# Convolution weights loaded in one order of the phases, the other order copied across the partition halves by ScalarE

## What is computed

```
t1 = p1_w * x ;  t2 = x + t1 ;  t4 = relu(x)
t5 = unfold(x, 3 x 7 taps, padding 1, 3)              # (n, c, 21, h, w)
t7 = einsum('oc,nchw->nohw', p7_w, t4)
t8 = unfold(t7, 1 x 5 taps, dilation 3, padding 6)
t9 = x[:, :, None] - t8
t10 = grouped 1x1 convolution of t2 by p10_w (4 groups, 32 -> 672 channels each)
t11 = einsum('nck,nmk->ncm', t1, t5) / sqrt(h * w)
t12 = t9.mean(2)
t13 = einsum('ncm,nmk->nck', t11, t10) / sqrt(c * 21)
out = maximum(t13, t12)
```

## Time and profile before

| | |
|---|---|
| median of 3 runs | 400.69 us (400.04 to 400.71) |
| the profiled execution | 400.21 us |
| its span, first to last instruction | 398.4 us |
| outside the span | 1.8 us |
| mean granted TensorE clock | 0.997 |
| TensorE, VectorE, ScalarE, GpSimd busy | 98%, 82%, 62%, 21% of the span |
| moved by DMA | 90.76 MB, 228 GB/s over the span |

### The profile page before, as it was taken

The page is one execution under the profiler, slowest core; times in us unless marked ns, Lnnn a source line. Parts: engine busy times, 40 slices in busy tenths (PEclk is TensorE's granted clock), DMA queues, the critical chain, the costliest instruction groups (busy, mean ns, idle before and its releaser), DMA issues.

```text
span 398.4 us, 10378 instructions
## 1 busy us (share of the span) xinstructions
PE 388.6 (98%) x4104; PEld 170.9 (43%) x4104; DVE 328.7 (82%) x395; ACT 249.0 (62%) x714; POOL 84.1 (21%) x72
## 2 busy tenths in 40 slices
PE   7999999999999999999999999999999999999995
PEld 3222653435633364333833337333553337332373
DVE  5988969988987897878978789787878789787625
ACT  1053547776577673776556773777727766578870
POOL 0442000522022221222022220222202222222200
PEclk9999999999999999999999999999999999999998
DMA  8999408893767949677566848579395783643205
GB/s 314 405 408 410 164 2 319 311 332 111 266 214 252 332 133 302 200 253 249 191 219 249 286 158 252 180 265 324 126 318 176 250 282 107 214 133 108 79 3 212
DMA packets 28705, 90.76 MB, mean 228 GB/s; under 512 B 3312, under 2 KB 3568, under 8 KB 28656
## 3 DMA queue, kind: packets, MB, share of 16 engines
q1 hardware_dynamic: 28656, 90.09, 64.1%
HBM read 73.30 MB, written 16.78 MB: 226 GB/s over the span
## 4 chain that ended last, share of the span: by engine, by line
PE 87%; ACT 4%; DVE 3%; DMA 2%; issue 2%; SPq 1%; DVEq 0%; ACTq 0%
PE ps_y L731 40%; PE ps_y L816 13%; PE ps_p L753 12%; PE ps_t L753 12%; PE ps_y L742 8%; ACT t L335 3%; DMA xw<-x_conv 2%; PE ps_y L753 2%; ACT base L273 1%; DVE yT L543 1%; DVE base L584 0%; DVE pair_sum L553 0%; SPq L170 0%; DVE box L561 0%; DVE box L570 0%
## 5 line engine op out<-in xcount | busy, mean ns | idle before, releaser
L731 PE MATMUL ps_y<-v_planes,u_planes 64*64 64x512 f32 x1536 | 193.0, 596 | 1.7 <-issue 0.7
L242 POOL TENSOR_TENSOR t1T<-t1T,p1T_sb 128x512 f32<-128x512 f32 x60 | 76.4, 1296 | 277.3 <-PE ps_y L742 245.4
L335 ACT ACTIVATE t<-xn,p_plus 128x64 f32<-128x64 f32 x512 | 128.0, 334 | 0.0
L753 PE MATMUL ps_p<-box,p_fifth 64*64 64x512 f32 x456 | 117.3, 590 | 0.5 <-DVE box L570 0.5
L753 PE MATMUL ps_t<-t,aT 64*64 64x512 f32 x448 | 115.4, 591 | 0.1
L731 PEld LDWEIGHTS ps_y<-v_planes,u_planes 64*64 64x64 f32 x1536 | 56.2, 132 | 116.3 <-issue 98.2
L273 ACT ACTIVATE base<-ps_p 128x512 f32<-128x512 f32 x57 | 34.0, 597 | 76.5 <-PE ps_p L753 76.1
L584 DVE TENSOR_TENSOR base<-ps_t,base 128x512 f32<-128x512 f32 x56 | 38.5, 688 | 27.9 <-PE ps_t L753 27.8
L816 PEld LDWEIGHTS ps_y<-t1T,yT 128*128 128x128 f32 x512 | 57.8, 192 | 6.5 <-issue 5.7
L816 PE MATMUL ps_y<-t1T,yT 128*128 128x128 f32 x512 | 59.3, 277 | 0.0
L543 DVE STREAM_TRANSPOSE yT<-ps_y 128x512 f32<-128x512 f32 x64 | 42.0, 695 | 17.5 <-PE ps_y L742 17.5
(11 more groups left out here) (43 smaller groups left out, 148.0 us busy)
## 6 DMA issues: line engine op xcount, KB each, us to landing
xw<-x_conv SPq DMA_DIRECT2D x64, 561.0 KB, 6.5
xn<-x_nat SPq DMA_DIRECT2D x32, 512.0 KB, 4.6
t1T<-x_pix SPq DMA_DIRECT2D x32, 512.0 KB, 6.8
out<-base SPq DMA_DIRECT2D x64, 256.0 KB, 4.9
u_planes<-w_tiles SPq DMA_DIRECT2D x4, 672.0 KB, 8.6
p1T_sb<-p1T SPq DMA_DIRECT2D x1, 128.0 KB, 10.7
p_sb<-p7T SPq DMA_DIRECT2D x1, 64.0 KB, 10.7
p_sb<-p SPq DMA_DIRECT2D x1, 32.0 KB, 11.0
```

The lines of the kernel that those rows point to most:

```text
L242: nc.gpsimd.tensor_tensor(part, part, p1T_sb[:, e, :].unsqueeze(1).broadcast_to([P, 4, C]), ALU.mult).then_inc(t1_ready, 1)
L335: last = nc.scalar.activation(t2[:, h, W * r:W * (r + 1)], xn[:, f, at:at + W], ACT.Copy, scale=p1_plus[:, 8 * h + r:8 * h + r + 1])
L731: last = nc.tensor.matmul(dst[TILE * pair:TILE * pair + TILE, :], weights_of(rows_of(half), u, weights, TILE * k, TILE), data_of(rows_of(h ...
L753: last = nc.tensor.matmul(dst[cols, 0:data.shape[-1]], weights[rows, cols], data[rows, :], start=start, stop=False, skip_group_check=True)
```

## The change

The weights come from memory in the FRONT order alone, three rows a group, into planes 0 to 2 of six (`U_0`, `U_2`, `OUTER`). `weights` makes three sums of 224 elements: `U_1` (as scratch) = r0 + r2, `U_1_FRONT` = that + r1, and `U_2` = that - r1, the last now behind a wait of its own. Then ScalarE copies the planes `OUTER` and `U_1_FRONT` of each half of the partitions into the planes `U_3` and `U_1` of the other half: two copies of 64 partitions x 448 elements a group (`swap`). TensorE waits for the copies (`u_swapped`) and no longer for the sums. One of the warm-up matmuls becomes half as long.

```diff
-U_0, U_2, U_1, U_3 = (FRONT, 0), (FRONT, 1), (BACK, 1), (BACK, 2)
+U_0, U_2, OUTER, U_1_FRONT, U_3, U_1 = range(6)
-        u_planes = sb("u_planes", [P, GROUPS, 2, KH, WCOLS])
+        u_planes = sb("u_planes", [P, GROUPS, 6, WCOLS])
-                sp.dma_start(u_planes[:, g], w_tiles[g]).then_inc(w_loaded[g], 16)
+                sp.dma_start(u_planes[:, g, 0:KH, :], w_tiles[g]).then_inc(w_loaded[g], 16)
...
-                both = u_planes[:, g].rearrange("p o r c -> p (o r) c")
-                nc.vector.tensor_tensor(both[:, 2:4], both[:, 0:4:3], both[:, 2:6:3], ALU.add).then_inc(u_steps, 1)
+                u = u_planes[:, g]
+                nc.vector.tensor_tensor(u[:, U_1], u[:, U_0], u[:, OUTER], ALU.add).then_inc(u_steps, 1)
                 dve.wait_ge(u_steps, U_STEPS * g + 1)
-                nc.vector.tensor_tensor(both[:, 4], both[:, 3], both[:, 4], ALU.add).then_inc(u_steps, 1)
-                nc.vector.tensor_tensor(both[:, 1], both[:, 2], both[:, 1], ALU.subtract).then_inc(u_steps, 1)
+                nc.vector.tensor_tensor(u[:, U_1_FRONT], u[:, U_1], u[:, U_2], ALU.add).then_inc(u_steps, 1)
+                dve.wait_ge(u_steps, U_STEPS * g + 2)
+                nc.vector.tensor_tensor(u[:, U_2], u[:, U_1], u[:, U_2], ALU.subtract).then_inc(u_steps, 1)
...
+            def swap(g):
+
+                if g < 2:
+                    act.wait_ge(u_steps, U_STEPS * (g + 1))
+                else:
+                    act.wait_ge(u_later, U_STEPS * (g - 1))
+                for half in range(2):
+                    copy(u_planes[TILE * half:TILE * half + TILE, g, U_3:U_1 + 1, :],
+                         u_planes[TILE - TILE * half:P - TILE * half, g, OUTER:U_1_FRONT + 1, :]).then_inc(u_swapped, 1)
...
+            swap(0)
+            swap(1)
             copy_two(0)
+            swap(2)
             copy_two(1)
             act.wait_ge(small_loaded, SMALL)
             copy(p7_fifth[:], p7_sb[:], FIFTH).then_inc(p7_scaled, 1)
             relu(0, 0)
+            swap(3)
             seed_x(0, 0)
...
-                        pe.wait_ge(u_steps, U_STEPS * (u + 1))
                     else:
                         pe.wait_ge(v_ready, 3 * u + 2)
-                        if u < GROUPS:
-                            pe.wait_ge(u_later, U_STEPS * (u - 1))
+                    if u < GROUPS:
+                        pe.wait_ge(u_swapped, 2 * u + 2)
...
-            for bank_set in (ps_p7[:, 0:HALF // 2], ps_t13, ps_p7, ps_p7):
+            for bank_set in (ps_p7[:, 0:HALF // 2], ps_p7[:, 0:HALF // 2], ps_t13, ps_p7):
```

More of the change, by code:

```diff
@@ L122, in conv_seq_kernel @@
         u_later = sem("u_later")
+        u_swapped = sem("u_swapped")
         v_ready = sem("v_ready")
@@ L247, in weights @@
                 pool.wait_ge(w_loaded[g], 16)
-                both = u_planes[:, g].rearrange("p o r c -> p (o r) c")
-                nc.gpsimd.tensor_tensor(both[:, 2:4], both[:, 0:4:3], both[:, 2:6:3], ALU.add).then_inc(u_later, 1)
+                u = u_planes[:, g]
+                nc.gpsimd.tensor_tensor(u[:, U_1], u[:, U_0], u[:, OUTER], ALU.add).then_inc(u_later, 1)
                 pool.wait_ge(u_later, U_STEPS * (g - 2) + 1)
-                nc.gpsimd.tensor_tensor(both[:, 4], both[:, 3], both[:, 4], ALU.add).then_inc(u_later, 1)
-                nc.gpsimd.tensor_tensor(both[:, 1], both[:, 2], both[:, 1], ALU.subtract).then_inc(u_later, 1)
+                nc.gpsimd.tensor_tensor(u[:, U_1_FRONT], u[:, U_1], u[:, U_2], ALU.add).then_inc(u_later, 1)
+                pool.wait_ge(u_later, U_STEPS * (g - 2) + 2)
+                nc.gpsimd.tensor_tensor(u[:, U_2], u[:, U_1], u[:, U_2], ALU.subtract).then_inc(u_later, 1)
             nc.gpsimd.memset(v_planes[:, :, :, 0:BLOCKS_PAD:BLOCKS_PAD - 1, :], 0.0).then_inc(edges_zeroed, 1)
@@ L719, in weights_of @@
             def weights_of(rows, u, plane, at, width):
-                order, row = plane
-                return u_planes[rows, u % GROUPS, order, row, at:at + width]
+                return u_planes[rows, u % GROUPS, plane, at:at + width]
             def data_of(rows, u, plane, block):
@@ L982, in weight_tiles @@
     w = p10.reshape(GROUPS, CG, KH, KW, CG)
-    out = np.zeros((GROUPS, P, 2, KH, WCOLS), p10.dtype)
+    out = np.zeros((GROUPS, P, KH, WCOLS), p10.dtype)
     for g in range(GROUPS):
-        for order in range(2):
-            for quarter, phase in enumerate(PHASES_OF[g % 2, order]):
-                rows = slice(CG * quarter, CG * quarter + CG)
-                for k, (pair, at) in enumerate(DENSE[phase <= 2]):
-                    for s in range(2):
-                        tap = phase + PHASES * (at - 1) - (2 * pair + s)
-                        out[g, rows, order, :, TILE * k + CG * s:TILE * k + CG * s + CG] = w[g, :, :, tap]
-                to, at = SINGLE[phase]
-                out[g, rows, order, :, 3 * TILE:] = w[g, :, :, phase + PHASES * (at - 1) - to]
+        for quarter, phase in enumerate(PHASES_OF[g % 2, FRONT]):
+            rows = slice(CG * quarter, CG * quarter + CG)
+            for k, (pair, at) in enumerate(DENSE[phase <= 2]):
+                for s in range(2):
+                    tap = phase + PHASES * (at - 1) - (2 * pair + s)
+                    out[g, rows, :, TILE * k + CG * s:TILE * k + CG * s + CG] = w[g, :, :, tap]
+            to, at = SINGLE[phase]
+            out[g, rows, :, 3 * TILE:] = w[g, :, :, phase + PHASES * (at - 1) - to]
     return out
```

## The result

With the change the kernel takes 398.84 us (median of 6 runs, 398.73 to 399.26), beside 400.41 us (median of 6) for the kernel before. The ratio is 0.9961, with a 95% interval of 0.9949 to 0.9974: about 1.6 us less, and faster by more than 0.2%. The profiled execution took 398.83 us against 400.21, with a span of 397.0 us against 398.4.

The account below looks back on a forecast made before the run. TensorE, busy 98%, was taken as the limit, its start bound by transferred bytes; 0.85 us at unit 0 plus 0.16 at unit 1 made 1.01 us off the 400.69 median: 399.7 us, range 398.9 to 400.6.

Parts of the forecast that it names:

- What bounds the start: First 20 us: TensorE's start waits on transfers and is bound by bytes, at 379 to 411 GB/s.
- The sums and copies, at nothing: VectorE sums end at 5.10, ScalarE's first copies at 6.2 us; the eight copies' 4.5 us fit idle time, costing nothing.
- The bytes, 0.85 us: One halved weight load ahead of unit 0's last data transfer brings that data 0.85 us earlier; upper bound 0.91.
- It does not hold up 7.64: Shortened warm-up leaves TensorE free at 7.26 us, so it does not delay unit 0's start at 7.64.
- Unit 0's term: Start of unit 0: TensorE begins its first weight load 0.85 us earlier.
- Unit 1's wait, 0.16 us: Start of unit 1: TensorE's 0.16 us of waiting for VectorE disappears as well.
- So nothing more is won: After the start: earlier transfers bring no further gain, since vector engines hardly wait for transfers from 14 to 62 us.
- moves with it: Later units: the vector engines' work is released by TensorE and shifts along with TensorE's earlier start.
- Rival 2: After unit 3 an engine not moving with TensorE ends last, gain given back: no change, 400.6 us; chance 0.12.
- The basis: Whole kernel: the gain was subtracted from 400.69 us, the median of the runs before, giving 399.7 us.
- Rival 1 and 3: Start: ramp or late clock trims gain, about 400.1 us (0.22); much later clock rise, slower (0.06, including a late copy).

Follow-up runs that it names:

- e1: Changed kernel with every weight load back at all six planes (672 KB); 400.43 us, ratio 1.0008 against the kernel before.
- e5: Changed kernel with only group 0's weight load at full 672 KB; median 400.05 us, ratio 1.0008 against the kernel before.
- e11: Changed kernel with only the weight loads of groups 2 and 3 at full size; 399.28 us, ratio 0.9965 against the kernel before.
- e7: Changed kernel with two more pairs of ScalarE copies, into a scratch buffer, ahead of each pair; 400.17 us, ratio 0.9998.
- e8: Changed kernel with 256 fewer warm-up columns and unit 0's last transfer and sum split into 9 and 8 blocks; 399.38 us, ratio 0.9989.
- e4: Changed kernel with another 256 columns of warm-up removed; 399.11 us, ratio 0.9973 against the kernel before.
- e2: Changed kernel with the longer warm-up of the kernel before (256 columns more); 399.37 us, ratio 0.9976.
- e3: Kernel before with only the shorter warm-up of the change; median 400.29 us, ratio 1.0008.
- e6: Changed kernel with only group 1's weight load at full size; 399.93 us, ratio 0.9983 against the kernel before.
- e10: Changed kernel with group 1's weight load moved behind the first half of unit 1's data; 399.57 us, ratio 0.9980.
- e12: Changed kernel with only group 0's weight load at full size and the long warm-up of before; 400.10 us, ratio 0.9991.
- e9: Changed kernel unaltered, timed again in a later series; 399.26 us, ratio 0.9968 against the kernel before.
- e18: Changed kernel with GpSimd's first two product pairs for image 1 released at other points, between VectorE's sums; 398.05 us, ratio 0.9944.

## Why the prediction was wrong, point by point

- **What bounds the start: right.** e1, e5 and e11 show that the gain is the bytes ahead of units 0 and 1 and nothing else; the chain's DMA share went from 2% to none.
- **The sums and copies, at nothing: right.** Forecast ends of 5.10 and 6.2, measured 5.08 and 6.29; two copies took 1.17 us against 1.1. GpSimd's sums were over at 15.15 (forecast 14.6 to 17.7). e7 shows the cover: about 1.05 us.
- **The bytes, 0.85 us: too small, and taken for one number.** V_1 began 1.09 us earlier (7.69 to 6.60). By the landings of the 16 parts, the first came 0.81 earlier (6.87 to 6.06), the eighth 0.94 (7.15 to 6.21) and the last 1.09 (7.67 to 6.58). The rate gave the first rightly; what VectorE waits for is the last. How much earlier the last comes isn't fixed by one pair of profiles: over all profiles but e8's, it came at 7.61 to 8.06 us with the full first load (7 profiles, middle one 7.77) and at 6.47 to 7.77 with the half (12 profiles, median 7.00), which is 0.77 between the medians, while the mean of the 16 parts came 0.96 earlier. So 1.09 is that of a good draw, and the sum below holds for this pair.
- **"It does not hold up 7.64" (the warm-up): too optimistic by a little.** It was to end at 7.26, and start unit 0 with V_1 at 7.64. Data came earlier than I thought, and then the warm-up did hold unit 0, by 0.06 us (e4). Unit 0's term is 1.03 us, not 0.85.
- **Unit 1's wait, 0.16 us: 0.24.** I took 1.08 us from the singles to the next unit out of later units; behind unit 0, which has half as many of them, it is 1.02 (10.67 to 11.69). The sum of the two terms is 1.27 us instead of 1.01.
- **"So nothing more is won", and it "moves with it": wrong.** 0.12 us more were won, at 70 us, where GpSimd's products met VectorE's sums otherwise. The fourteen profiles with the products at their place sort by one number, how long before `pair_sum` they start: from 0.02 us before it to 0.36 behind (the changed kernel, e2, e3, e5, e6, e7, e10, e11) `pair_sum` takes 1.31 or 1.32 us and the way 21.51 to 21.53; from 0.08 to 0.16 before it (the kernel before, e1, e4, e12) 2.40 us and 21.65 or 21.66; over 2 us before it (e8, e9) 2.40 us and 22.2 or 22.3. So the 0.12 us come from a shift of 0.06 us, and not from the change as such. "What these engines do is released by TensorE and moves with it" failed: GpSimd's products there were released by a transfer (`t1T<-x_pix`), and moved by 1.21 us where TensorE moved by 1.27. In e9 they even began at 68.06 us, although TensorE was 1.16 us later than in the first profile. Rival 2 (gain given back) did not come about between the first two profiles, where TensorE's lead never shrinks. But e9 shows it in the same program: a lead of 0.12 us at unit 1 had become a lag of 0.54 at 81 us.
- **The basis, the largest single part.** I set the forecast on 400.69 us, the median of three runs. With more runs the kernel before is at 400.3 to 400.4 (400.41 beside the change). That is 0.28 us of the 0.84 by which 399.68 was too high; 0.37 are the terms above (1.38 between the profiled executions, not 1.01); the remaining 0.19 are that the profile before lay 0.20 below its own median and the one after only 0.01. The miss of the range, 0.06 us, is smaller than the scatter: e9, the same kernel, gave 399.26 us, inside the range.
- **Rival 1 and 3 (the clock): not in the changed kernel's profile** (loads 0.43 apart from 7.94 on), but the clock is a real price next to it: e1, e3, e5, e7 and e8 pay some 1.3 to 2.4 us for it in 1 to 5 of their 11 or 12 runs. Only e8's profile shows the rise itself too late, as both rivals had it; in those of e3 and e7 the level had risen and was lost in the pause, which neither rival had. That this would hit kernels whose data come late, and not this one, whose real work follows the warm-up at once, I had only half seen.

The way the change works was right; the failure is one of size. The steps that failed are "I take 0.85" (unit 0 began 1.03 us earlier), the "0.16 us of waiting" behind it (0.24), "nothing more is won" (0.12 were) and "The median of the runs is 400.69" as the number to take the gain from (400.41 with six runs). With the 0.19 us between profiles and medians they add up to the 0.84 us.

## What to carry to other kernels

Where a start is bound by transfers, count the bytes ahead of the first operand that the bottleneck waits for; halving a load that stands there is worth its time even if another engine must rebuild the other half, as long as that work has slack (here about 1.05 us). The length of a warm-up is tied to when the real work starts: move one, move the other, and look at the spread of runs as well as at the median. An engine far off the critical path can still cost more than the change at hand, by where its work falls beside VectorE's (e18: some 0.8 us for two waits moved): look there before shaving the start further.

## What the runs showed of the hardware

- **One late part delays a transfer.** In e6, e9 and e10 the last of the 16 parts of unit 0's second half came 0.95 to 1.24 us after the 15th, in e18 0.67, in the other profiles with one piece 0.01 to 0.26 us (landing records of the trace). It began between the two halves of unit 0's data, and the next loads behind it had a late part again (e9: 1.12, 1.04 and 1.06 us). In e8 the first half had it already, 1.06 us. Why a part falls behind was not tried; it stays open, and with it whether a different split could avoid it. In e9 it cost 1.15 us at the start (unit 1 at 12.84 instead of 11.69), and the meeting at 70 us 0.8 more: that is how one program comes to 398.83 and to 400.76 us.
- **The clock level's rise moves about.** The trace's record of the granted clock begins with the rise; the windows ahead of it read 1.00, while the records stand at the pace of 1.2 GHz. It rose at 7.07 us before and at 7.27 us after the change, and in e1 to e12 anywhere from 5.2 (e7) to 8.3 us (e5), in e8 at 11.0, with the warm-up starting at 2.2 us in all. Where it came at 8.06 us (e11), unit 0's first step took 0.61 us instead of 0.48. The Trainium skill, "TensorE: Matmul & The Clock Gate", Part 1, gives the variation as some 500 ns either way; here it was three times as much, e8 aside.
- **It also falls again in a pause.** In e3 the level rose at 5.75 us, TensorE stood still from 6.8 to 8.8 us, and the level was lost at 9.16, when it had just begun to work. In e7 it rose at 5.22, TensorE stood still from 6.5 to 8.6, and the level was lost at 8.64. These are the two longest pauses ahead of unit 0 in all profiles (2.0 and 2.1 us). e12 and e18 paused for 1.6 us and e4 for 1.3, with rises as early (5.35, 5.36 and 5.29), and lost nothing. What decides between them wasn't tried.
- **VectorE's sums of two SBUF operands beside a GpSimd product** took 2.40 us instead of 1.32, 2.18 instead of 1.23 and 1.79 instead of 0.72, and GpSimd's pair 3.55 instead of 2.52 (e18). Its sums with a PSUM operand and its transposes ran in their usual 0.68 and 1.31 us beside the same products. A start that differs by 0.06 us decides which sum is hit.
